# Making the relative term's chunks in pairs at half as many places of a unit

## The reference

```
q, k, v = heads of (x @ Wq + bq), (x @ Wk + bk), (x @ Wv + bv)
scores  = q . k                                   # 1024 x 1024 per head and sequence
rel     = q . rel_key[p]                          # p = 0..255
bias    = rel at clip(j - i + 255, 0, 255)
logits  = (scores + bias) * 8 ** -0.5,  -inf where j > i
out     = softmax(logits) @ v, then @ Wo + bo
```

## Time and profile before

| what | us |
| --- | --- |
| median of 3 runs (872.11 to 877.11) | 875.83 |
| the profiled execution | 875.68 |
| its span | 874.0 |
| TensorE busy in the span | 681.4 (78%) |
| VectorE busy | 609.4 (70%) |
| ScalarE busy | 547.7 (63%) |
| GpSimd busy | 205.8 (24%) |
| exponentials, L976, 288 of them | 287.2 |
| score matmuls, L797, 960 | 177.3 |
| chunk matmuls, L818, 2048 | 86.3 |

### The profile page before, as it was taken

One profiled execution on the slowest core, in us unless ns is written; L12 is line 12 of the kernel. 1 busy time (PEld: TensorE's weight loads), 2 busy tenths in 40 slices (PEclk: granted clock), 3 DMA queues, 4 the chain that ended last, 5 costly groups with the idle time before them and its releaser, 6 DMA issues. The chain is left out here.

```text
span 874.0 us, 15422 instructions
## 1 busy us (share of the span) xinstructions
PE 681.4 (78%) x6144; PEld 401.8 (46%) x6144; DVE 609.4 (70%) x1177; ACT 547.7 (63%) x653; POOL 205.8 (24%) x115
## 2 busy tenths in 40 slices
PE   0686623888889898888888988987459978889884
PEld 0333212444444344444444434434347766767573
DVE  6699932667767667677676766764957598678754
ACT  0355512777877777777877777785446838656473
POOL 8133418044071160440803506200000000000000
PEclk9887765899999899999999999998778999989997
DMA  5333662014123041131221412202300001000000
GB/s 66 75 101 113 173 195 36 28 35 106 56 57 84 28 105 35 48 93 56 64 77 29 111 50 61 58 1 68 114 1 6 21 0 49 1 1 24 1 24 25
DMA packets 38900, 49.68 MB, mean 57 GB/s; under 512 B 7330, under 2 KB 30450, under 8 KB 36402
## 3 DMA queue, kind: packets, MB, share of 16 engines
q1 hardware_dynamic: 38826, 48.66, 21.4%
HBM read 36.71 MB, written 11.94 MB: 56 GB/s over the span
## 5 line engine op out<-in xcount | busy, mean ns | idle before, releaser
L976 ACT ACTIVATE probs<-p_s 128x1024 f32<-128x1024 f32 x288 | 287.2, 1027 | 122.4 <-DVE p_s L903 48.4
L797 PE MATMUL p_s<-q_sb,k_sb 96*128 96x384 bf16 (+2 forms) x960 | 177.3, 307 | 40.4 <-ACT probs L976 37.7
L903 DVE TENSOR_TENSOR p_s<-p_s,even_b 128x512 f32<-128x512 f32 (+1 forms) x160 | 125.5, 802 | 77.8 <-PE p_s L797 63.0
L841 PE MATMUL p_o<-probs,v_sb 128*32 128x128 f32 (+3 forms) x1920 | 162.3, 448 | 0.9 <-ACT o_acc L995 0.4
L797 PEld LDWEIGHTS p_s<-q_sb,k_sb 96*128 96x128 bf16 x960 | 70.0, 100 | 151.2 <-ACT probs L976 82.0
L760 POOL TENSOR_SCALAR_AFFINE_SELECT even_b<-even_b 128x2048 f32<-128x2048 f32 x32 | 75.4, 2358 | 247.6 <-ACT even_b L988 241.8
L1353 PE MATMUL p_z<-hid_hi,h_hi 128*128 128x512 f32 x256 | 104.8, 409 | 8.7 <-ACT hid_hi L1454 4.4
L818 PE MATMUL p_s<-q_rows,rel_w 72*128 72x64 bf16 x2048 | 86.3, 199 | 30.1 <-ACT probs L976 22.3
L818 PEld LDWEIGHTS p_s<-q_rows,rel_w 72*128 72x128 bf16 x2048 | 76.8, 102 | 61.0 <-ACT probs L976 31.7
L1356 PE MATMUL p_z<-hid_lo,h_hi 128*128 128x512 f32 x256 | 104.1, 407 | 0.0
L915 DVE TENSOR_TENSOR p_s<-p_s,odd_b 128x512 f32<-128x512 f32 x96 | 65.1, 695 | 43.6 <-PE p_s L797 43.5
(11 more groups left out here) (149 smaller groups left out, 818.9 us busy)
## 6 DMA issues: line engine op xcount, KB each, us to landing
k_sb<-k_dram SPq DMA_DIRECT2D x48, 192.0 KB
q_sb<-q_dram SPq DMA_DIRECT2D x16, 576.0 KB
q_rows<-qr_dram SPq DMA_DIRECT2D x42, 192.0 KB
q_dram<-q_parts SPq DMA_DIRECT2D x12, 256.0 KB, 3.3
k_dram<-k_parts SPq DMA_DIRECT2D x12, 256.0 KB, 3.4
qr_dram<-q_turned SPq DMA_DIRECT2D x12, 256.0 KB, 3.6
x_all<-in_L_attn_x_dram SPq DMA_DIRECT2D x4, 512.0 KB, 4.4
h_nat<-in_L_ffn_h_w_dram SPq DMA_DIRECT2D x2, 1024.0 KB, 8.6
```

Of the source, the lines that this page charges most:

```text
L797: last = nc.tensor.matmul(slot[:, c:c + n * BLK], k_sb[hg][:, h * S + j * BLK:h * S + (j + 1) * BLK], ap(q_sb[hg], at, [[HG * S, KROWS], [ ...
L841: last = nc.tensor.matmul(p_o[32 * h:32 * h + 32, at:at + blocks * BLK], v_sb[hg][:, j, h * 32:(h + 1) * 32], probs[n % PBUFS][:, h, col * ...
L903: last = nc.vector.tensor_tensor(cols, cols, even_term(h, NEAR[g], run), ALU.add)
L976: nc.scalar.activation(probs[m % PBUFS][:, hp * 2:hp * 2 + 2, :].rearrange("p h c -> p (h c)"), p_s[SLOT_OF["scores", n]][:, :], ACT.Exp, ...
```

## The change

The chunks are made two at a time. Odd chunks stood singly behind steps 0, 2, 4, 7, 9, 12, 14 and 16, and now stand in pairs behind steps 1, 5, 10 and 15. Even chunks stood behind 20, 21, 23, 24, 26, 27, 29 and 30, and now in pairs behind 20, 23, 26 and 29. In each pair the first chunk is copied by VectorE and the second by ScalarE; of the even chunks ScalarE had copied 1, 4 and 6 and now copies 1, 3, 5 and 7. The slots follow from the new order by the same rule. The remaining edits make the loops of each queue go over a pair.

```diff
-    ODD_AT = {0: 0, 2: 1, 4: 2, 7: 3, 9: 4, 12: 5, 14: 6, 16: 7}
-    EVEN_AT = {20: 0, 21: 1, 23: 2, 24: 3, 26: 4, 27: 5, 29: 6, 30: 7}
+    ODD_AT = {1: (0, 1), 5: (2, 3), 10: (4, 5), 15: (6, 7)}
+    EVEN_AT = {20: (0, 1), 23: (2, 3), 26: (4, 5), 29: (6, 7)}
     ACT_ODD = {1, 3, 5, 7}
-    ACT_EVEN = {1, 4, 6}
+    ACT_EVEN = {1, 3, 5, 7}
...
             got.append(("scores", u * STEPS + k))
-            if k in ODD_AT:
-                got.append(("odd", u * FILL + ODD_AT[k]))
-            if k in EVEN_AT and u < NU - 1:
-                got.append(("even", (u + 1) * FILL + EVEN_AT[k]))
+            got += [("odd", u * FILL + c) for c in ODD_AT.get(k, ())]
+            if u < NU - 1:
+                got += [("even", (u + 1) * FILL + c) for c in EVEN_AT.get(k, ())]
...
-                    if k in ODD_AT:
-                        copy_fill("odd", u * FILL + ODD_AT[k])
-                    if k in EVEN_AT and u < NU - 1:
-                        copy_fill("even", (u + 1) * FILL + EVEN_AT[k])
+                    for c in ODD_AT.get(k, ()):
+                        copy_fill("odd", u * FILL + c)
+                    for c in EVEN_AT.get(k, ()) if u < NU - 1 else ():
+                        copy_fill("even", (u + 1) * FILL + c)
```

More of the change, by code:

```diff
@@ L867, in _ @@
                     scores(u, k)
-                    if k in ODD_AT:
-                        relative("odd", u * FILL + ODD_AT[k])
-                    if k in EVEN_AT and u < NU - 1:
-                        relative("even", (u + 1) * FILL + EVEN_AT[k])
+                    for c in ODD_AT.get(k, ()):
+                        relative("odd", u * FILL + c)
+                    for c in EVEN_AT.get(k, ()) if u < NU - 1 else ():
+                        relative("even", (u + 1) * FILL + c)
                     if u > 0:
```

## The result

The changed kernel takes **898.56 us** (897.74 to 899.92, four runs) against 875.88 for the one before: a ratio of 1.0268 (95% interval 1.0234 to 1.0302), so 2.7% slower. Forecast were 906 us and a range of 880 to 930. The profiled execution has a span of 898.1 us, 24.1 more than before.

A forecast was written before the change was run, and what follows sets the result against it. No engine was full; the ring of three slots between engines was taken as the bound. 875.7 us plus 17.1 for the ring and 14 for clock falls gave 906.8, forecast as 906 us, range 880 to 930.

The forecast's parts named there:

- The pair's price: Odd half: exponentials after the pairs at steps 1, 5, 10, 15 come 2.47, 2.78, 3.04 and 3.35 us after the one before.
- S6: TensorE's score matmuls of step 6, behind the pair of step 5; forecast to wait for step 5's exponential to end.
- e5: ScalarE's exponential of step 5; the next was forecast 2.78 us after it, behind the pair of step 5.
- The odd half: Unit's stretch from the exponential of step 0 to that of step 19: 31.94 us against 29.70, +2.24 us each.
- The even half: Stretch from step 19's exponential to the next unit's first: 25.59 us against 25.71 before, -0.12 us each.
- The ring term: Whole loop: longer waits for slots in eight odd and seven even halves, +17.1 us.
- The clock term: Attention loop: 19 falls of TensorE's clock against 9, each 1.4 us, +14 us; bounds 0 and +42.
- rival 3: Attention loop: the longer slot waits hold but clock falls stay at nine, 893 us; chance 0.25.
- Rival 4: Attention loop: a clock fall at nearly every drained pair, 935 us; chance 0.13.
- Rival 1: Attention loop: only the work counts, a pair costs less than two singles, 15 us won, 861 us; chance 0.09.
- My reading of the values groups: Pairs of steps 10 and 15: a values group right behind a pair delays the next exponential further, 0.57 us each.
- the replay: Unit worked entry by entry with traced durations, taking the later of engine and slot; 57.5 us for the change.

The follow-up runs named there:

- after: The changed kernel itself, all chunks made in pairs, against the kernel before; 898.56 us, ratio 1.0268.
- even_pairs: Kernel before with only the even chunks paired (behind 20, 23, 26, 29) and ScalarE copying 1, 3, 5, 7 of them; 879.6 us, 1.0049 times before.
- odd_next: Kernel before with odd chunks behind steps 1, 2, 5, 6, 10, 11, 15, 16, each pair's second one step later; 885.4 us, 1.0129 times before.
- odd_gap: Kernel before with odd chunks behind steps 1, 3, 5, 7, 10, 12, 15, 17, each pair's second two steps later; 880.6 us, 1.0057 times before.
- values_away: Changed kernel with two values groups moved off the pairs of steps 10 and 15 to steps 9 and 14; 884.7 us, 1.0084 times before.
- opt_b: Changed kernel with another new order of chunk places, ScalarE's copies and values groups, holding two pairs and a group of three; 832.0 us, 0.9520 times before.
- before_filled: Kernel before with the matmuls of odd chunk 6 and of the scores of step 24 issued twice; 865.6 us, 0.9898 times before.
- opt_a: Changed kernel with a new order of chunk places, ScalarE's copies and values groups, holding two pairs and a group of three; 844.4 us, 0.9657 times before.
- after_filled: Changed kernel with the matmuls of four chunks per unit and of the scores of steps 15 and 20 issued twice; 893.5 us, 1.0221 times before.

## Why the prediction was right, step by step

- **The bound.** Right: not an engine but the ring of three slots. after, even_pairs, odd_next, odd_gap, values_away and opt_b have the same work to within a copy, and their full units at full clock take from 51.1 to 57.9 us.
- **The pair's price, 2.47, 2.78, 3.04 and 3.35 us.** Traced in the changed kernel: 2.51, 2.85, 3.11, 3.54. The wait is the forecast one: S6 starts 0.06 us after e5's end. The odd half, taking each interval where it ran at full clock, sums to 31.9 us, forecast 31.94, against 29.70 before.
- **The even half, -0.12.** Of the wrong sign: 25.7 at least by intervals and 26.0 by the full unit (57.92 - 31.9) against 25.71 before, so +0.3. The pairs of 20 and 26 take 2.84 and 2.97, replayed 2.75 and 2.84. even_pairs puts it at 0.1 to 0.4.
- **The ring term, +17.1.** It was +19.4: six full units at 57.92 - 55.41 = 2.5, and about 2.2 each for the first and the last, taken at equal falls.
- **The clock term, +14.** Mis-sized. Four more falls (13 against 9) at 1.53 are +6.2 us; 19.4 + 6.2 is the 25.6 us by which the loop grew. The price per fall (forecast 1.4) was right. The count was not: I took 0.6 falls for each idle of 1.17 and more and 0.3 for those of about 1.05. The idles themselves came out shorter: behind the pairs of steps 1, 5, 10 and 15 they are 0.77, 0.95, 0.84 and 1.22 us, where 1.04, 1.17, 1.06 and 1.32 were forecast, and the long one of the even half is 1.19, not 1.34. That leaves 14 of 1.17 and more in the loop, not 23, and one fewer than before. Nor does the rule hold: values_away, with as many idles over 0.6 us as the changed kernel (36 in six units in either trace), has two falls. This sum is where 906 and 898.6 part, and rival 3 (893, no more falls) and the forecast lay on either side of what came. Rival 4's 935 lies above the range that was said to take in most of it, and nothing came near it. It was luck that the total came as near: the ring was taken 2.3 us too small and the clock 7.8 too large.
- **Nothing from owners, masks and reloads.** Right by even_pairs for the first; the stages around the loop moved by 1.5 us in all, of which no part is explained here.
- **Rival 1, faster by overlapping the copies.** The prediction and this rival both had the two copies of a pair side by side, and that was misread. Each engine's copy stands behind its own part of the step, and the exponential starts when the add ends. In the unit from 331.81 the two records overlap by 0.3 us or less, and in two of its eight pairs not at all. Both copies are free all the same, as the prediction counted them: VectorE's runs beside the exponential, ScalarE's in the wait for the next. The rival failed since neither engine was what the loop waited for. The Trainium skill (PSUM — Partial Sum Buffer, "Specifications (TRN2)") says that the two engines reach PSUM in parallel at full bandwidth where their banks differ. The trace agrees where the copies do meet: in the pair with the longest overlap, 0.61 us at 196.19, they take 1.22 and 1.02 us, as they do alone.
- **My reading of the values groups** behind the pairs of steps 10 and 15 as an own price of 0.57 each was wrong as an account, though the replay's sum was right: values_away moved them and the ring stayed at 57.9.

What stays open is what decides where the clock falls. The kernels here say only that it is not the longest idle, and that with little extra work in front of the two longest idles (before_filled) there was one fall and not nine.

## What to carry to other kernels

When a few buffers go round between engines in a fixed order, read the order as a ring: for each entry ask which instruction frees its buffer, and how far ahead of it the filling engine then is. Replay that with traced durations before moving anything; here it gave every kernel's full unit at full clock to within 1 us in 51 to 58, but for opt_a's, which it had 1.9 us too short. And look at the granted clock unit by unit before taking a small difference for an effect of the order, since two kernels with the same ring differed by 14 us and had 2 and 13 falls.

## What the runs showed of the hardware

- Issuing matmuls twice made a kernel 1% faster: before_filled issues 16 chunk matmuls and 4 score matmuls more per unit and takes 865.6 us against 874.4 in the same comparison, as TensorE fell to 1.2 GHz once in the loop and not nine times.
- With idles of 0.95 and 1.31 us in each of five units the granted clock stayed at 2.4 GHz (values_away), and with one of 1.51 in four units of opt_a; with the same 0.95 idle it fell in the changed kernel (unit at 0.94).
- Falls can repeat with the loop: five units of odd_gap take 58.04 to 58.05 us with two falls each.
- A fall made a unit 1.1 to 1.5 us longer: 58.96 against 57.88 us in values_away with one, 60.98 against 57.92 in after_filled with two.
